# The self and cross attentions of layer 1 as one rotating loop, with their products in small tiles of the array

## What is computed

```python
x = rms_norm(h, ln_in_w)
q, k, v = split(where(vm, x @ v_qkv, x @ l_qkv), 3)     # 16 heads of 16, then rotary on q and k
ctx = softmax(causal(q k^T / 4)) v                      # self attention, per head, 128 x 128
h = h + where(vm, ctx @ v_dense, ctx @ l_dense)         # two experts, vm chooses by token
cq = rms_norm(h, w) @ cq_w ; ck, cv = split(encoder @ ckv_w, 2)   # 16 heads of 8
h = h + (softmax(cq ck^T / sqrt(8)) cv) @ cdense_w      # cross attention
h = h + where(vm, mlp_v(rms_norm(h)), mlp_l(rms_norm(h)))
```

## Time and profile before

| | kernel before |
|---|---|
| median of 3 runs | 1572.76 us |
| the profiled execution | 1576.42 us, span 1574.5 us |
| PE busy | 1472.0 us (93%), 10850 products |
| PE weight loads | 1242.7 us (79%) |
| DVE / ACT / POOL busy | 914.9 (58%) / 706.8 (45%) / 370.1 us (24%) |
| chain that ended last | PE 62%, issue 20%, POOL 8%, DVE 7%, ACT 2% |
| mean granted TensorE clock | 0.975 |

### The profile page before, as it was taken

The page is one execution under the profiler, slowest core; times in us unless marked ns, Lnnn a source line. Parts: engine busy times, 40 slices in busy tenths (PEclk is TensorE's granted clock), DMA queues, the critical chain, the costliest instruction groups (busy, mean ns, idle before and its releaser), DMA issues.

```text
span 1574.5 us, 31313 instructions
## 1 busy us (share of the span) xinstructions
PE 1472.0 (93%) x10850; PEld 1242.7 (79%) x10850; DVE 914.9 (58%) x2003; ACT 706.8 (45%) x2277; POOL 370.1 (24%) x472
## 2 busy tenths in 40 slices
PE   5889899899989989999998999998998999999899
PEld 4757676767767768999987888887987788887899
DVE  3546664655655677566545555656663555556664
ACT  2324344334433446222246665566335565566432
POOL 0135323324414420000003222331011222223100
PEclk9999999999999988999999999999998999999999
DMA  4203000000000002000010000001000100000000
GB/s 154 67 20 114 4 1 3 3 0 0 7 0 1 1 1 88 1 0 0 1 54 5 5 7 3 3 1 60 28 0 1 59 7 3 3 3 1 5 23 27
DMA packets 13226, 30.21 MB, mean 19 GB/s; under 512 B 2400, under 2 KB 8800, under 8 KB 12512
## 3 DMA queue, kind: packets, MB, share of 16 engines
q1 hardware_dynamic: 13152, 29.23, 5.3%
HBM read 27.13 MB, written 2.10 MB: 19 GB/s over the span
## 4 chain that ended last, share of the span: by engine, by line
PE 62%; issue 20%; POOL 8%; DVE 7%; ACT 2%; DMA 0%; SPq 0%; POOLq 0%; DVEq 0%; ACTq 0%
PE bank L828 55%; PE bank L841 7%; POOL p L1736 2%; POOL xT L1736 1%; POOL kbd L1736 1%; POOL rstd L1694 1%; DVE pT L1209 1%; DVE stats L1239 1%; DVE nmax L1310 1%; DVE xn L1285 1%; POOL kbd L1727 1%; DVE xn L1289 0%; DVE xn L1287 0%; DVE x_all L1342 0%; DMA p<-in_media 0%
## 5 line engine op out<-in xcount | busy, mean ns | idle before, releaser
L1548 ACT ACTIVATE p<-bank,nmax 128x128 f32<-128x128 f32 x512 | 146.8, 370 | 261.2 <-DVE nmax L1310 260.8
L1310 DVE TENSOR_REDUCE nmax<-bank 128x4 f32<-128x512 f32 x256 | 170.3, 686 | 130.0 <-PE bank L828 129.6
L828 PE MATMUL bank<-w_ff_rounded,hT_rounded 128*128 128x256 f32 x944 | 218.1, 286 | 7.4 <-ACT w_ff_rounded L1658 2.6
L1209 DVE COPY pT<-bank 128x512 f32<-128x512 f32 x256 | 169.7, 683 | 90.3 <-PE bank L841 89.8
L828 PE MATMUL bank<-kbd,hT 64*128 64x128 f32 (+1 forms) x1280 | 203.6, 340 | 5.0 <-ACT hT L1493 3.9
L828 PE MATMUL bank<-xT_rounded,w_ff_rounded 128*128 128x256 f32 x864 | 197.2, 286 | 3.7 <-issue 2.4
L828 PE MATMUL bank<-xT_rounded,kbd_rounded 128*128 128x256 f32 x608 | 173.5, 285 | 0.0
L828 PE MATMUL bank<-xn_rounded,w_ff_rounded 128*128 128x256 f32 x608 | 172.9, 284 | 0.0
L828 PEld LDWEIGHTS bank<-w_ff_rounded,hT_rounded 128*128 128x128 f32 x944 | 163.5, 193 | 9.1 <-ACT v L1493 3.0
L841 PEld LDWEIGHTS bank<-consts,p 128*128 128x128 f32 x784 | 94.5, 143 | 77.1 <-issue 69.4
L828 PEld LDWEIGHTS bank<-xT_rounded,w_ff_rounded 128*128 128x128 f32 x864 | 149.8, 193 | 5.1 <-issue 5.1
(11 more groups left out here) (160 smaller groups left out, 3071.9 us busy)
## 6 DMA issues: line engine op xcount, KB each, us to landing
ctxT<-in_ctxT SPq DMA_DIRECT2D x32, 128.0 KB, 2.4
w_ff<-in_w1b SPq DMA_DIRECT2D x6, 640.0 KB, 6.6
w_att<-in_w2a SPq DMA_DIRECT2D x1, 3072.0 KB, 10.9
w_att<-in_w3a SPq DMA_DIRECT2D x1, 3072.0 KB, 10.2
w_att<-in_w1a SPq DMA_DIRECT2D x1, 2432.0 KB, 11.1
hT<-in_xT SPq DMA_DIRECT2D x8, 256.0 KB, 3.0
o<-in_x SPq DMA_DIRECT2D x8, 256.0 KB, 3.1
w_ff<-in_w2b SPq DMA_DIRECT2D x1, 2048.0 KB, 7.8
```

The lines of the kernel that those rows point to most:

```text
L828: return pe.matmul(dst, lhsT, rhs, start=first, stop=last)
L1209: dve.tensor_copy(dst, src).then_inc(sems[s[0], "copied"], 1)
L1310: dve.tensor_reduce(nmax[:, ph.place[s] % P_RING, :], bank[:, :].rearrange("p (h t) -> p h t", h=QUAD), AX_X, ALU.max, negate=True).then_i ...
L1548: t = act.activation(p[:, part], bank[:, part], ACT.Exp, bias=nmax[:, i, j:j + 1])
```

## The change

Phase 1 is rewritten after the pattern of the media attentions, and what it touches follows.

- **Loop.** `gated_slots` and `gated_sides` replace `attention` and the old weave: 16 slots per iteration, each a pair of groups. Slot k holds the mix (the new values step) of pair k-4, the turns of pair k-3, the scores of pair k and the share of pair k-1, all modulo 16: the loop is rotated. The order is cross A, self A (of the next iteration), cross B, self B (of the next iteration). So the first half iteration of self attention moves ahead of the loop, and the last cross attentions behind it.
- **Scores.** Self pairs stand on array rows 0 to 63 and 64 to 127, cross pairs on two neighbouring strips of 32 rows; each is still 512 moving columns. The keys are spread over four head rows only: POOL writes 128x512 per (sequence, half) for self and 128x512 per sequence for cross, 12 instructions per iteration in place of 16 of 128x1024.
- **Softmax.** ACT accumulates the sums with the exponentials; DVE inverts them once for a pair; POOL multiplies the probabilities (2 of 128x512 for a pair). The division after the values goes.
- **Values.** `mix`: the values are stationary, padded to 32 columns, in four column tiles, with 128 moving columns of transposed probabilities; 8 products (16 records) for a pair. The context comes out transposed, ACT copies it (`ctx`, `coT`). The steps `mask`, `maskedT` and the transposes of `coT` go.
- **Dense.** Both experts' weights are the moving operand of one product of 512 columns; DVE adds the two halves with the mask as a scalar (2 instructions per sequence). `cdense` is split by sequence. `qT`/`kT` become `qkT` by sequence, with two copies on ACT.
- **Banks.** Four banks for scores, one for all mixes, three for everything else.
- **Setup.** The cross weight `cdense` is loaded in 16 pieces of 8 rows, so there are 16 more DMA issues at the start; POOL clears the whole of `v`; DVE has two small extra instructions. Norms of the later layers share one set of semaphores (`norm_ln`), which moves no work.

```diff
+def gated_slots():
+    quads = [("cross", A_, 0), ("self", A_, 1), ("cross", B_, 0), ("self", B_, 1)]
+    pairs = [((kind, u, b, c), early) for kind, u, early in quads for b in range(ROWS) for c in range(GROUPS // 2)]
+    n = len(pairs)
+    def of(k, steps):
+        pair, early = pairs[k % n]
+        return [(s, early + k // n) for s in steps(*pair)]
+    def mix(kind, u, b, c):
+        done = [({"self": "ctx", "cross": "coT"}[kind], u, b)] if c == GROUPS // 2 - 1 else []
+        return [(of_kind("mix", kind), kind, u, b, c)] + done
     slots = []
-    for i in range(len(groups) + SKEW_O):
-        slot = []
-        if i < len(groups):
-            slot += here(("scores",) + groups[i])
-        if 0 <= i - SKEW_T < len(groups):
-            slot += here(("turn",) + groups[i - SKEW_T])
-        if 0 <= i - SKEW_O < len(groups):
-            slot += here(("values",) + groups[i - SKEW_O])
-        slots.append(slot)
+    for k in range(n):
+        slots.append((of(k - 4, mix) + of(k - 3, lambda *pair: groups_of("turn", pair)),
+                      of(k, lambda *pair: groups_of("scores", pair))
+                      + of(k - 1, lambda *pair: groups_of("share", pair)[0:1])))
     return slots
+def gated_sides():
+    def part(u):
+        v, of_v = (B_, here) if u == A_ else (A_, ahead)
+        keys_a, keys_b = (ahead(*spreads("self", u)[b * DC:(b + 1) * DC]) for b in range(ROWS))
+        keys_c = of_v(*spreads("cross", v))
+        return [(ahead(("norm_self", u)), [], ahead(("scale_self", u))),
+                ([], ahead(("xvT", u), ("xlT", u)), []),
+                ([], [], ahead(("qk", u, 0), ("qk", u, 1), ("qkT", u, 0)) + keys_a[:1]),
+                ([], of_v(("dense", v, 0)) + keys_a[1:], of_v(("dense", v, 1), ("norm_cross", v))),
+                ([], ahead(("v1", u)) + of_v(("scale_cross", v)) + ahead(("qkT", u, 1)) + keys_b, []),
+                ([], of_v(("nT", v), ("ck", v)), keys_c[:1]),
+                ([], [], here(("cdense", u, 0), ("half", u))),
+                ([], of_v(("cv", v), ("cq", v)) + keys_c[1:], here(("cdense", u, 1), ("end", u)))]
+    return part(A_) + part(B_)
+def gated_body():
+    return [front + first + early + second + late
+            for (first, second), (front, early, late) in zip(gated_slots(), gated_sides())]
...
+        first = [s for slot in gated_body() for s in slot if s[1]]
+        n = first.index((("qkT", A_, 0), 1))
+        return of_a + end_a + half(B_, first[:n], []) + end_b + first[n:]
...
+    slots = gated_body()
+    if pre[0] == ("xvT", A_):
+        return [s for slot in slots for s in slot]
+    of_this = [[s for s in slot if not s[1]] for slot in slots]
+    n = len(of_this)
+    return weave(of_this, (ahead(*norms[0:2]), n // 2 + 1, n // 2 + 2), (ahead(*norms[2:]), n // 2 + 4, n // 2 + 5),
+                 (ahead(*pre), n - 1, n - 1))
...
+        if index == 1:
+            of_scores = [s for s in jobs if s[0].startswith("scores")]
+            mixes = [s for s in jobs if s[0] in ("mix", "mix_cross")]
+            others = [s for s in jobs if s not in of_scores + mixes]
+            self.bank = {s: i % QUAD for i, s in enumerate(of_scores)} | {s: BANKS - 1 for s in mixes}
+            self.bank |= {s: QUAD + i % (BANKS - QUAD - 1) for i, s in enumerate(others)}
...
-            sp.dma_start(w_att[:, 0:W1A_COLS], dram["w1a"]).then_inc(weights_att, 16)
+            at = W1A["cdense"][0]
+            sp.dma_start(w_att[:, 0:at], dram["w1a"][:, 0:at]).then_inc(weights_att, 16)
+            for j in range(QUAD):
+                for n in range(GROUPS):
+                    to, row_at = j * STRIP + n * HDC, (n * QUAD + j) * HDC
+                    sp.dma_start(w_att[to:to + HDC, at:at + D], dram["w1a"][row_at:row_at + HDC, at:at + D])\
+                      .then_inc(weights_att, 16)
...
+            def scores_gated(ph, it, s):
+                name, kind, u, b, g = s
                 w = views[u]
-                heads = slice(g * QUAD, (g + 1) * QUAD)
+                banks = [ps[ph.bank[s[:4] + (g + i,)]] for i in range(2)]
                 if kind == "self":
-                    pe.wait_ge(*after(ph, it, ("qT", u), "copied"))
-                    pe.wait_ge(*after(ph, it, ("spread", kind, u, b, g // 2), "done"))
-                    mm(bank[:, :], ident16[:, :], causal16[:, :].unsqueeze(1).broadcast_to([P, QUAD, P]), True, False)
-                    t = mm(bank[:, :], w.qT1[:, b, g // 2, :], w.k1[:, b, heads, :], False, True)
-                elif kind == "cross":
+                    c = g // 2
+                    pe.wait_ge(*after(ph, it, ("qkT", u, b), "copied"))
+                    pe.wait_ge(*after(ph, it, ("spread_self", u, b, c), "done"))
+                    settle(pe, "tensor")
+                    for bank in banks:
+                        mm(bank[:, :], ident16[:, :], causal16[:, :].unsqueeze(1).broadcast_to([P, QUAD, P]), True, False)
+                    for i, bank in enumerate(banks):
+                        part = slice(i * HD2, (i + 1) * HD2)
+                        mm(bank[:, :], w.qT1[part, b, c, :], w.k1[part, b, c, :, :], False, True).then_inc(sems[name, "mm"], 1)
+                else:
                     pe.wait_ge(*after(ph, it, ("cq", u), "copied"))
-                    pe.wait_ge(*after(ph, it, ("spread", kind, u, b, g // 2), "done"))
-                    t = mm(bank[:, :], w.cqT[:, b * P:(b + 1) * P], w.k1[:, b, heads, :], True, True)
-                t.then_inc(sems[s[0], "mm"], 1)
+                    pe.wait_ge(*after(ph, it, ("spread_cross", u, b), "done"))
+                    settle(pe, "tensor")
+                    for i, bank in enumerate(banks):
+                        part = slice((g + i) * STRIP, (g + i + 1) * STRIP)
+                        mm(bank[:, :], w.cqT[part, b * P:(b + 1) * P], w.ck1[part, b, :, :], True, True)\
+                            .then_inc(sems[name, "mm"], 1)
...
+            def mix(ph, it, s, bank):
+                kind, u, b, c = s[1:]
+                pe.wait_ge(*after(ph, it, (of_kind("turn", kind), kind, u, b, 2 * c + 1), "copied"))
+                pe.wait_ge(*after(ph, it, ("v1" if kind == "self" else "cv", u), "copied"))
+                for i in range(2):
+                    for j in range(QUAD):
+                        strip = slice(j * STRIP, (j + 1) * STRIP)
+                        if kind == "self":
+                            head = 2 * j + i
+                            t = mm(bank[strip, c * P:(c + 1) * P], v_strip(kind, u, b, c * HDC + head),
+                                   pT_ring[head // QUAD][:, head % QUAD * P:(head % QUAD + 1) * P], i == 0, i == 1)
+                        else:
+                            group = 2 * c + i
+                            t = mm(bank[strip, 0:P], v_strip(kind, u, b, group * QUAD + j), pT_ring[i][:, j * P:(j + 1) * P],
+                                   group == 0, group == GROUPS - 1)
                 t.then_inc(sems[s[0], "mm"], 1)
...
-                            t = mm(bank[:, b * D:(b + 1) * D], views[u].oT1[:, b, e, c, :],
-                                   weight(w_att, W1A, f"dense{e}")[:, c, :], e + c == 0, e + c == 2)
+                at, chunks, width = W1A["dense0"]
+                both = w_att[:, at:at + EXPERTS * chunks * width].rearrange("p (e c n) -> p c e n", e=EXPERTS, c=chunks)
+                pe.wait_ge(*after(ph, it, ("ctx", u, b), "copied"))
+                for c in range(DC):
+                    t = mm(bank[:, :], views[u].ctxT[:, b, c, :], both[:, c, :, :], c == 0, c == DC - 1)
...
+                kind, u, b, g = s[1:]
+                dve.wait_ge(*after(ph, it, (of_kind("scores", kind), kind, u, b, g + 1), "exp"))
+                dve.reciprocal(rshare[:, g:g + 2, :], rsum[:, g:g + 2, :]).then_inc(sems[s[0], "rinv"], 1)
...
+                for e, event in enumerate(("half", "added")):
+                    if e:
+                        dve.wait_ge(*after(ph, it, s, "half"))
+                    dve.scalar_tensor_tensor(out=x_b, in0=bank[:, e * D:(e + 1) * D].unsqueeze(1),
+                                             scalar=vm_here[:, u, b, e:e + 1], in1=x_b,
+                                             op0=ALU.mult, op1=ALU.add).then_inc(sems[s[0], event], 1)
...
+                act.wait_ge(*after(ph, it, ("spread_self", u, b, DC - 1), "done", back=1))
+                act.wait_ge(*after(ph, it, s, "mm"))
+                act.activation(views[u].k_flat[:, b * D:(b + 1) * D], bank[:, D:2 * D], ACT.Copy).then_inc(sems[s[0], "flat"], 1)
+                act.activation(views[u].qT1[:, b, :, :], bank[:, 0:D].rearrange("p (c t) -> p c t", c=DC), ACT.Copy,
+                               scale=HD1 ** -0.5).then_inc(sems[s[0], "copied"], 1)
...
+                    t = act.activation(p[:, part], bank[:, part], ACT.Exp, bias=nmax[:, g, j:j + 1],
+                                       accum_out=rsum[:, g, j:j + 1])
...
+            def spread_self(ph, it, s, bank):
```

(7 more changed lines are left out.)

326 lines of the change are left out of this document (140 added, 186 removed), and 4 rows, old and new, of the table EVENTS.

## The result

The median falls from 1574.36 us (1571.05 to 1577.66) to **1508.16 us** (1501.73 to 1510.82): the ratio is 0.9574, with a 95% interval from 0.9536 to 0.9611, 4.3% faster. The profiled executions took 1576.42 and 1501.73 us. The forecast was 1488 us, its own range 1470 to 1508 and the whole range 1450 to 1532: the median lies at the upper end of the first.

A forecast was written before the change was run, and what follows sets the result against it. PE's own work was taken to bound phase 1: -101 us of work and +16 us of idle make -85 us, from 1576.4 to 1491.4 profiled, median 1488 us. Own range 1470 to 1508 (58%), whole range 1450 to 1532.

The forecast's parts named there:

- Scores: Phase 1 scores, two groups on different array rows: 27.5 us per iteration to 17.8, -9.7 us; bounds 13.8 and 21.4.
- Mix: Values step in four column tiles: 0.75 us a pair (0.6 to 1.02), 25.9 us per iteration to 12.0, -13.9 us.
- The sum of PE's work: PE's work in phase 1: -25.2 us per iteration, -101 us over four iterations.
- Idle: PE's idle time in phase 1: 47 us after against 31 before, +16 us, from loop, start and end.
- The wait for `xvT`: Second slot of each unit: PE waits for `scale_self`, 3.4 us idle, twice per iteration.
- The clock: Granted clock in phase 1: its present loss kept, ±15 us.
- From profile to median: Whole kernel: profiled execution forecast at 1491.4 us, the median 3.7 us lower, 1488 us.
- DVE, ACT, POOL: Busy time per iteration: DVE 66 to 70 us, ACT about 60, POOL about 56; none a bound by its sum.
- (a): Float32 score records start in strict program order, a pair lasting 1.29 us instead of 0.86: +27 us, 1515; 10%.
- (b): In-order DVE and POOL set the pace, each slot's chain late by a further 0.6 us: +38 us, 1526; 17%.
- (c): The 32-row and 32-column tiles take turns instead of running side by side: +132 us, 1620; 4%.
- (d): Everything at its lower bound: mix at 0.6 us, changes of form mostly hidden, half the new idle: 1458; 11%.

The follow-up runs named there:

- (7): Changed kernel plus 20 bf16 products of 256 columns that compute nothing, ahead of PE's wait for `scale_self`; same result: 1485.1 us.
- (10): Changed kernel with POOL's probability multiplication in phase 1 on 8 of 128 columns, so probabilities are not normalised: 1467.9 us.
- run 1: Changed kernel with the scores of phase 1 on all 128 array rows, summing the wrong heads: 1510.9 us.
- run 4: Changed kernel with the mix products of one tile next to each other in program order; same result: 1502.5 us.
- 2: Changed kernel with the mix in two 64-column tiles in place of four of 32; wrong contexts: 1515.3 us.
- run 3: Changed kernel with scores on all 128 rows and every mix product in one 32-column tile, nothing side by side; wrong result: 1569.3 us.
- 9: Changed kernel with scores on all 128 rows and 20 filler products ahead of the wait for `scale_self`; wrong result: 1505.8 us.
- run 11: Changed kernel with one POOL multiplication, in the slot behind the norm, held back until `scale_self` is done: 1504.8 us.

## Why the prediction was right, and where it was off

**Scores: right.** A cross pair takes 1.06 us, from 253.25 to the next full product at 254.31, which is the 0.86 of one group plus two changes of form at 0.10; a self pair behind its mask takes 1.06 as well. A change of form is the drain that the prediction cited from the Trainium skill, "TensorEngine Tiling (Array Packing)", Key Properties. The trace agrees as far as a time can: the pairs cost the 0.10 us a change that was read from the media scores. Two small sums in the prediction are off: the bound at twice the price comes to 21.8 and not 21.4, and the loop's idle time to 2 x 3.4 + 2 = 8.8 us and not 8.6.

```profile
253.25 1.13 PE L885 MATMUL bank<-kbd,hT 32*128 32x512 f32 x4
254.31 1.98 PE L885 MATMUL bank<-w_att,hT 128*128 128x512 f32 x4
...
262.14 1.13 PE L885 MATMUL bank<-kbd,hT 64*128 64x512 f32 x4
263.20 0.64 PE L885 MATMUL bank<-pT,v 128*32 128x128 f32 x16
```

**Mix: too dear.** 0.57 us where 0.75 was taken from the range 0.6 to 1.02, so even the lower bound was too high. 0.18 x 64 = 11.5 us more are gained. The records of four tiles start about twice as densely as those of two (0.57 against 1.07), which the text left open.

**The sum of PE's work: -99.8 against -101, and partly luck.** The mix alone would make it -112. What offsets it is the cut: the forecast started both kernels at 124 us, but of the records of `w_att,xT` with 512 columns 32 (14.1 us) stand ahead of that in before and 16 (7.1 us) in after; the others now lie behind it. Counted from 16 us the work falls by 111.0 us, as the cheaper mix wants it (the clock's two digits leave 3 to 4 us either way). An iteration by itself: 116.47 x 0.97 = 113.0 before, 91.64 x 0.95 = 87.1 after, -25.9 where the cheaper mix would make -28.1; for these 2 us there is no row.

**Idle: right in sum behind 124 us, 48.3 against 47, but not in its parts, and not in all.** The two iterations idle 6.3 and 6.4 us (8.6 forecast), the stage up to 226 us 13.4 (9 forecast for the start), that from 478.6 us 19.0 (12 forecast). In the last the cross pairs of B wait 4.0 us for exponentials once, and 2.0 and 2.5 in front of a mix. The wait for `xvT` came as described, twice per iteration, at 2.3 us where 3.4 was forecast. Its first instance, 8.15 us at 92 to 100 us where `w_ff` products used to stand, the forecast didn't have: from 16 us on, idle grows by 24.2 us and not by 16. So the work is 10 us better and the waits 8 us worse than forecast, and the two hide each other.

**The clock: the step that failed.** "I keep its present loss" was written of a change that put a new wait of 2 to 3 us into every unit, and in the same breath the text said that the loss rests on idle stretches which grow by a half. It grew by 10.2 us (22.8 to 33.0), with the stage ahead by 14.0, within the ±15 but near its end: the likely direction was known and the value was not moved. In the loop it takes the `xvT` wait: with the wait filled (7) or mostly gone (10) there is no 1.2 GHz stretch. How long a stretch gets behind an equal wait depends on something more (3.4 to 10.2 us in after, 0 to 3.4 in run 1).

**From profile to median.** 10 of the 20 us are the profile's (1491.4 against 1501.73): the clock's 14, less the 2 by which the work gained more than the waits lost and the 1.9 outside. The other 10 are the step to the median: the forecast subtracted 3.7 us, by which the profiled run of before lay above its median; the profiled run of after lies 6.4 us under its own. That is the clock too: its mean over the kernel was 0.964 in the profiled execution and 0.957 to 0.959 in the other three, which times the length is an estimate of 8 us.

**DVE, ACT, POOL: right, DVE a little high.** 62.8, 58.1 and 55.5 us per iteration against 66 to 70, about 60 and about 56. The iterations of 103 and 98 us enclose the forecast of 102; the first product of phase 2 came at 538.46, not 525.

**The rivals.** (a) falls: a pair has 1.06 us where strict order would need 1.29 and more, and run 4 rules it out for the mix. In this the trace disagrees with the rule from the Trainium skill, "TensorE: Matmul & The Clock Gate", section The mechanism, that was cited for it. (b) is present on a small scale: whenever PE got more work (runs 1, 2, 3 and 9), 10.5 to 27.5 us of idle went away, so the short slots are partly set by what DVE and ACT deliver. It doesn't have the 0.6 us a slot that (b) needed. (c) falls by run 3. (d): its price for the mix came true and its halved idle did not.

**What stays open.** Full rows without filler (run 1) lose 11.5 us to the clock, not 33, though the waits for `xn` are equally long (16.3 us against 15.8). Fuller products behind the wait, or the shorter waits elsewhere, could do that; no run parts the two. Nor does a run tell why equal waits in after are followed by 3.4, 6.8 or 10.2 us. How much of the gain of run 10 belongs to the one multiplication beside `scale_self` was not tried again after run 11 had missed it. The wait of 8.15 us ahead of 124 us was not tried either: putting the `w_ff` products back in front of `xvT` there would be the edit.

## What to carry to other kernels

Price a new wait of TensorE with what follows it: here 2.2 to 2.6 us of waiting brought 3.4 to 10.2 us at 1.2 GHz, 1.7 to 5.1 us more. Before a dense loop gains from smaller tiles, its waits have to go, or be filled; 10 to 20 products that compute nothing made this kernel 23 us faster, where the row tiles alone brought nothing. When work is taken away from the bounding engine, expect a part of it back in waits (a fifth to a third here) and perhaps more in the clock (21.5 of 38 us in run 1). Begin a split at a point ahead of which both kernels have done the same work. And when a step is moved away from a wait, look first whose queue makes it wait.
